# Layer 2 of a fused four-layer graph network: y as two float32r halves, one product of 256 columns per block

## The reference, cut to what matters

```
edge_emb = edge_attr @ We + be
edge_agg = segment_sum(edge_emb, dst, num_segments=num_nodes)
x_comb = concatenate([x, edge_agg], axis=-1)
neigh = segment_sum(x_comb[src], dst, num_segments=num_nodes)
h = x_comb + neigh
return relu(h @ W1 + b1) @ W2 + b2
```

## Time and profile before

| | us |
|---|---|
| median of 3 runs | 6356.68 (6347.64 to 6359.1) |
| the profiled execution | 6362.92 |
| its span, first to last instruction | 6357.5 |
| layer 2, first to last product of L1090 | 3405.5 to 4234.8 |
| first gather of layer 3 | 4248.8 |

### The profile page before, as it was taken

The page is one execution under the profiler, slowest core; times in us unless marked ns, Lnnn a source line. Parts: engine busy times, 40 slices in busy tenths (PEclk is TensorE's granted clock), DMA queues, the critical chain, the costliest instruction groups (busy, mean ns, idle before and its releaser), DMA issues.

```text
span 6357.5 us, 76532 instructions
## 1 busy us (share of the span) xinstructions
PE 5116.0 (80%) x25981; PEld 3920.8 (62%) x25981; DVE 2600.6 (41%) x10082; ACT 1910.0 (30%) x3903; POOL 3110.5 (49%) x3243
## 2 busy tenths in 40 slices
PE   6999999989999999999999999974454444444454
PEld 4777777757777777777776888854444444444344
DVE  7777777623333333333332111113343444434344
ACT  5777777622222222222222111111111111111112
POOL 0000000067777777777770000027777777777775
PEclk8999999999999999999999999987777777777777
DMA  3333322367777666666663555532222222222221
GB/s 135 126 126 126 125 121 122 126 199 210 207 207 209 204 203 204 207 203 203 205 205 116 179 179 177 177 112 54 55 55 54 55 55 54 55 54 55 54 55 44
DMA packets 466448, 844.29 MB, mean 133 GB/s; under 512 B 72324, under 2 KB 300212, under 8 KB 454548
## 3 DMA queue, kind: packets, MB, share of 16 engines
q1 hardware_dynamic: 322996, 509.22, 23.7%
q0 software_dynamic: 128960, 320.44, 18.3%
q10 hardware_dynamic: 14112, 9.74, 0.5%
HBM read 683.93 MB, written 155.18 MB: 132 GB/s over the span
## 4 chain that ended last, share of the span: by engine, by line
PE 65%; POOL 19%; issue 7%; DVE 4%; DMA 2%; ACT 2%; ACTq 0%; SPq 0%; POOLq 0%; DVEq 0%
POOL ring L485 19%; PE bank L970 16%; PE bank L1090 11%; PE bank L957 10%; PE bank L662 10%; PE bank L646 4%; PE bank L531 3%; DMA ring<-htab,src 2%; PE bank L1363 1%; PE bank L1399 1%; PE bank L1392 1%; PE bank L897 1%; PE bank L1370 1%; DVE ring L1294 1%; PE bank L894 1%
## 5 line engine op out<-in xcount | busy, mean ns | idle before, releaser
L485 POOL DMA_INDIRECT ring<-ptab,src x1612 | 1525.0, 946 | 1810.2 <-DMA ptab<-pO 1285.2
L485 POOL DMA_INDIRECT ring<-htab,src x1612 | 1580.9, 981 | 1398.8 <-DMA htab<-hs 907.9
L970 PE MATMUL bank<-ring,oh 128*126 128x384 f32 x3224 | 1218.8, 489 | 0.0
L926 DVE TENSOR_TENSOR ring<-bank,ring 128x512 f32<-128x512 f32 x806 | 553.0, 691 | 1397.1 <-PE bank L957 1150.2
L957 PE MATMUL bank<-w1e,ea 128*128 128x256 f32 x3224 | 833.4, 381 | 16.4 <-DVE ring L926 10.1
L940 ACT ACTIVATE ring<-ring 128x1024 f32<-128x1024 f32 x403 | 425.5, 1056 | 1229.0 <-DVE ring L926 1229.0
L957 PEld LDWEIGHTS bank<-w1e,ea 128*128 128x128 f32 x3224 | 614.4, 191 | 279.1 <-DVE ring L926 19.9
L1355 PE MATMUL bank<-ident,pk 128*72 128x128 f32 x90 | 38.3, 426 | 883.0 <-ACT pk L1317 883.0
L970 PEld LDWEIGHTS bank<-ring,oh 128*126 128x126 f32 x3224 | 590.3, 188 | 218.6 <-issue 0.6
L1399 PE MATMUL bank<-ring,oh 128*126 128x132 f32 x3224 | 576.1, 313 | 174.0 <-DVE ring L1294 171.7
L1399 PEld LDWEIGHTS bank<-ring,oh 128*126 128x126 f32 x3224 | 486.5, 213 | 254.6 <-DVE ring L1294 233.3
(11 more groups left out here) (254 smaller groups left out, 5865.3 us busy)
## 6 DMA issues: line engine op xcount, KB each, us to landing
ring<-ea_r SPq DMA_DIRECT2D x403, 256.0 KB, 4.0
ea<-ea_t SPq DMA_DIRECT2D x403, 256.0 KB, 3.1
atab<-ring SPq DMA_DIRECT2D x45, 1543.5 KB, 5.2
atab<-at SPq DMA_DIRECT2D x45, 1543.5 KB, 5.2
ring<-atab SPq DMA_DIRECT2D x54, 787.5 KB, 4.3
ring<-atab SPq DMA_DIRECT2D x54, 756.0 KB, 4.2
at<-atab SPq DMA_DIRECT2D x36, 787.5 KB, 4.3
at<-atab SPq DMA_DIRECT2D x36, 756.0 KB, 4.1
```

What stands on the lines that cost most here:

```text
L485: return e.indirect_dma_start(o, None, table, bass.IndirectOffsetOnAxis(ap=src[:, t:t + 1], axis=0))
L926: e.tensor_tensor(group1(gi, m % 2), MLP[m % 3][:, :].rearrange("p (g f) -> p g f", g=2), group1(gi, m % 2), ALU.add).then_inc(s_edge, 1)
L970: e.matmul(SUM[s % 2][0:SL, 0:384], slots_of(s, i), rv1[:, t // G % NR1, t % G, :], start=i == 0, stop=t == END[s]).then_inc(s_sum1, 1)
```

## The change

Layer 2 alone is changed.

- y is written as two halves of 12 bits in float32r, `yhl`, 256 columns of a block. `split2` does it on DVE alone, three instructions for each of the nine chunks: u = 4097 y - y, hi = 4097 y - u (rounded), lo = y - hi. Before it was two on DVE and two on ACT.
- Each of the 4410 products has 256 columns for 384, and both its operands are float32r.
- The adjacency is loaded in three parts of 17, 17 and 15 blocks, still bf16, into four buffers `adjb`, and each part is copied to float32r in one of three buffers `adj`: 270 copies. `by_vector` gives the odd ones from the fifth on to DVE (133), the others to ACT (137). A copy stands 11 places ahead of its first product. It waits for its load and for the last product of the part three before it. The load of a part waits for the copy of the part four before it.
- A group is kept with one ACT copy of 128 columns (for 256) and one DVE sum (for two).
- The new buffers lie over `ring`, `oh` and beyond, so that POOL clears `oh` (128 x 4788) behind the last sum of layer 2 (`pool2`), ahead of its gathers for layer 3, and DVE waits for that before layer 3.

```diff
@@ -115,8 +115,10 @@
     CMID = S * NB // 2
     CB = 6
     NCB = -(-NB // CB)
-    HALF = -(-NB // 2)
-    NAT = 5
+    THIRD = -(-NB // 3)
+    PARTS = [min(THIRD, NB - THIRD * k) for k in range(3)]
+    NAT = 4
+    SPLIT = 4097.0
     assert max(LAST[t] - FIRST[t] for t in range(NT)) <= 1 and max(B1[s] - B0[s] for s in range(NS)) <= 1
     assert (NRING * G) % GT == 0
     END = [min(GT * s + GT, NT) - 1 for s in range(NS)]
...
@@ -195,6 +195,10 @@
         flag = sb("flag", [P, 8])
         flagi = sb("flagi", [1, 1], I32)
         gidx = sb("gidx", [P, 2], I32)
+        held = sb("held", [P, ND, 384])
+        gathering = ExitStack()
+        ring = sb("ring", [P, NRING * G * HROW], c=gathering)
+        oh = sb("oh", [P, 2, GT * (SL + S)], c=gathering)
...
@@ -449,6 +454,13 @@
             w3h = sb("w3h", [P, 3, 4], c=l3)
             part = sb("part", [P, 2, P], c=l3)
             l3.close()
+            gathering.close()
+            halves2 = ExitStack()
+            yhl = sb("yhl", [P, NB, 256], FR, c=halves2)
+            adj = sb("adj", [P, 3, THIRD * SL], FR, c=halves2)
+            adjb = sb("adjb", [P, NAT, THIRD * SL], BF, c=halves2)
+            over = sb("over", [P, 2, CB * P], c=halves2)
+            halves2.close()
...
@@ -978,23 +987,58 @@
             N2, _, NODES2, KEEPS2, ADDS2, W2 = places(
                 0, (8, 14, 20, 26, 32, 33, 34, 35, 36, 42, 48, 54, 60, 62), GT, 64)
 
+            def by_vector(u):
+                return u > 3 and u % 2 == 1
+
+            def full2(u):
+
+                v = by_vector(u)
+                return s_full2v if v else s_full2a, sum(by_vector(w) == v for w in range(u + 1))
+
+            FULL2 = {}
+            for u in range(3 * NS):
+                FULL2.setdefault(max(0, GT // 3 * u - 11), []).append(u)
+
+            def pool2(e):
+
+                e.wait_ge(s_sum2, 3 * NS)
+                e.memset(oh[:, :, :], 0.0).then_inc(s_clear2, 1)
+
             def sync2(e):
                 e.wait_ge(s_sum1, NT)
                 e.wait_ge(s_mlp, 2 * NG)
-                for u in range(2 * NS):
+                for u in range(3 * NS):
                     if u >= NAT:
-                        e.wait_ge(d2.sum, u - NAT + 1)
-                    c, n = u % 2 * HALF * SL, (HALF if u % 2 == 0 else NB - HALF) * SL
-                    e.dma_start(PARTS[u % NAT][:, 0:n], atab[u // 2 * P:(u // 2 + 1) * P, c:c + n]).then_inc(
+                        e.wait_ge(*full2(u - NAT))
+                    c, n = u % 3 * THIRD * SL, PARTS[u % 3] * SL
+                    e.dma_start(adjb[:, u % NAT, 0:n], atab[u // 3 * P:(u // 3 + 1) * P, c:c + n]).then_inc(
                         s_part2[u % NAT], 16)
 
-            def y2(b):
-                return hs[:, b, 0:128]
+            def part_ready(e, u):
+                e.wait_ge(s_part2[u % NAT], 16 * (u // NAT + 1))
+                if u >= 3:
+                    e.wait_ge(s_sum2, u - 2)
+                n = PARTS[u % 3] * SL
+                return adj[:, u % 3, 0:n], adjb[:, u % NAT, 0:n]
+
+            def split2(e, c):
+
+                b = slice(CB * c, min(CB * c + CB, NB))
+                y, hi, lo = hs[:, b, 0:128], yhl[:, b, 0:128], yhl[:, b, 128:256]
+                u = over[:, c % 2, 0:(b.stop - b.start) * P].rearrange("p (b f) -> p b f", f=P)
+                e.wait_ge(s_yout1, b.stop)
+                if c >= 2:
+                    e.wait_ge(s_split2, 3 * c - 4)
+                e.scalar_tensor_tensor(out=u, in0=y, scalar=SPLIT, in1=y, op0=ALU.mult, op1=ALU.subtract).then_inc(s_split2, 1)
+                e.wait_ge(s_split2, 3 * c + 1)
+                e.scalar_tensor_tensor(out=hi, in0=y, scalar=SPLIT, in1=u, op0=ALU.mult, op1=ALU.subtract).then_inc(s_split2, 1)
+                e.wait_ge(s_split2, 3 * c + 2)
+                e.tensor_tensor(lo, y, hi.bitcast(F32), ALU.subtract).then_inc(s_split2, 1)
 
             def vector_post2(e, b, k):
                 n, x, o = 5 * b, xs[:, b, :], tail1(b)
                 if k == 0:
-                    e.wait_ge(d2.add, b + 1)
+                    e.wait_ge(s_add2, b + 1)
                     if b:
                         e.wait_ge(s_turn2, b)
                     e.tensor_tensor(mS[:, 0:128], acc1(b, 128), hs[:, b, 0:128], ALU.add).then_inc(s_in2, 1)
...
@@ -1056,22 +1100,33 @@
             def vector2(e):
                 e.wait_ge(s_sum1, NT)
                 for q in range(N2):
-                    dense_split_v(e, d2, q, y2)
+                    if q < NCB:
+                        split2(e, q)
+                    for u in FULL2.get(q, []):
+                        if by_vector(u):
+                            e.tensor_copy(*part_ready(e, u)).then_inc(s_full2v, 1)
                     if q - 1 in KEEPS2:
-                        thirds_added(e, d2, KEEPS2[q - 1])
+                        s = KEEPS2[q - 1]
+                        h = held[0:SL, s % ND, :]
+                        e.wait_ge(s_low2, s + 1)
+                        e.tensor_tensor(h[:, 128:256], SUM[s % 2][0:SL, 0:128], h[:, 0:128], ALU.add).then_inc(s_kept2, 1)
                     if q in NODES2:
-                        node_hots(e, NODES2[q], d2.node, d2.add, ND, B1[max(0, NODES2[q] - ND)] + 1)
+                        node_hots(e, NODES2[q], s_node2, s_add2, ND, B1[max(0, NODES2[q] - ND)] + 1)
                     for b, k in W2.get(q, []):
                         vector_post2(e, b, k)
 
             def scalar2(e):
                 e.wait_ge(s_sum1, NT)
                 for q in range(N2):
-                    if q % 2 == 0 and q // 2 < NCB:
-                        e.wait_ge(s_yout1, min(CB * (q // 2) + CB, NB))
-                    dense_split_a(e, d2, q, y2)
+                    for u in FULL2.get(q, []):
+                        if not by_vector(u):
+                            e.activation(*part_ready(e, u), ACT.Copy).then_inc(s_full2a, 1)
                     if q in KEEPS2:
-                        thirds_kept(e, d2, KEEPS2[q], 384, 2 * KEEPS2[q] + 2)
+                        s = KEEPS2[q]
+                        e.wait_ge(s_sum2, 3 * s + 3)
+                        if s >= ND:
+                            e.wait_ge(s_add2, B1[s - ND] + 1)
+                        e.activation(held[0:SL, s % ND, 0:128], SUM[s % 2][0:SL, 128:256], ACT.Copy).then_inc(s_low2, 1)
                     for b, k in W2.get(q, []):
                         scalar_post2(e, b, k)
 
@@ -1080,19 +1135,19 @@
                 for q in range(N2):
                     g, i = q // GT, q % GT
                     for h in range(NB * i // GT, NB * (i + 1) // GT) if g < NS else ():
-                        u, c = 2 * g + h // HALF, h % HALF
+                        u, c = 3 * g + h // THIRD, h % THIRD
                         if c == 0:
-                            e.wait_ge(s_part2[u % NAT], 16 * (u // NAT + 1))
+                            e.wait_ge(*full2(u))
                         if h == 0 and g >= 2:
-                            e.wait_ge(d2.kept, 2 * (g - 1))
+                            e.wait_ge(s_kept2, g - 1)
                         if g == 0 and h % CB == 0:
-                            e.wait_ge(d2.lo, 2 * (h // CB) + 2)
-                        m = e.matmul(SUM[g % 2][0:SL, 0:384], PARTS[u % NAT][:, c * SL:c * SL + SL], ysp[:, h, 0:384],
+                            e.wait_ge(s_split2, 3 * (h // CB) + 3)
+                        m = e.matmul(SUM[g % 2][0:SL, 0:256], adj[:, u % 3, c * SL:c * SL + SL], yhl[:, h, :],
                                      start=h == 0, stop=h == NB - 1)
-                        if h in (HALF - 1, NB - 1):
-                            m.then_inc(d2.sum, 1)
+                        if c == PARTS[u % 3] - 1:
+                            m.then_inc(s_sum2, 1)
                     for b in LASTS.get(ADDS2.get(q), []):
-                        add_nodes(e, b, 128, 128, d2.node, d2.kept, 2, s_in2, 1, d2.add)
+                        add_nodes(e, b, 128, 128, s_node2, s_kept2, 1, s_in2, 1, s_add2)
                     for b, k in W2.get(q, []):
                         tensor_post2(e, b, k)
 
...
@@ -1283,6 +1338,7 @@
 
             def vector3(e):
                 e.wait_ge(s_hout2, NB)
+                e.wait_ge(s_clear2, 1)
                 for u in range(NS + 8):
...
@@ -1400,7 +1456,7 @@
                                      stop=t == END[g]).then_inc(s_sum3, 1)
 
             with nc.Block() as block:
-                block.gpsimd(lambda e: [f(e) for f in (pool1, pool3)])
```

More of the change, by code:

```diff
@@ L146, in build @@
         atab = nc.dram_tensor("atab", [NS * P, NB * SL], BF)
-        ring = sb("ring", [P, NRING * G * HROW])
         src = sb("src", [P, NT], I32)
@@ L159, in build @@
         npcol = sb("npcol", [P, NB])
-        oh = sb("oh", [P, 2, GT * (SL + S)])
         oh2 = sb("oh2", [P, ND, 256])
@@ L405, in expected @@
             s_eat = [sem(f"s_eat{i}") for i in range(NEA)]
-            d0, d2 = (Dense(*(sem(f"s_{n}{i}") for n in Dense._fields)) for i in (0, 2))
```

(21 more changed lines are left out.)

## The result

| | before | after |
|---|---|---|
| median, us | 6355.3 (4 runs, 6347.64 to 6359.1) | 6166.6 (4 runs, 6165.89 to 6168.08) |
| span of the profiled execution, us | 6357.5 | 6160.6 |
| layer 2, first to last product, us | 829.3 | 635.5 |
| last product to first gather of layer 3, us | 14.0 | 18.15 |

The changed kernel takes 0.9705 of the time before, with a 95% interval of 0.9688 to 0.9722: 189 us less by the medians, 197 by the two profiled spans. The forecast was 6132 us. A second set of four runs on another chip gave 0.9700 (0.9684 to 0.9716).

A forecast was written before the change was run, and what follows sets the result against it. PE alone was taken to bound layer 2: products -237, opening +1, steps and weights +11 make -225 us from the profiled 6362.9, so 6138; the median 6.2 lower, 6132 us. Range 6105 to 6210.

The forecast's parts named there:

- one pass with small stalls: Forecast's main case for layer 2: float32r products in one pass and few waits, 6105 to 6162 us; chance 67%.
- (d): Rival: layer 2's copies and block steps bind, by stalls of 40 us and a slower DVE cast: 6162 to 6192 us; 11%.
- (e): Rival: layer 2's transfers bind, if 210 to 230 GB/s is the most: 6166 to 6225 us; 6%.
- The product: Layer 2's 4410 products: one float32r pass of 110 ns in place of 163.7, saving 237 us.
- (a): Rival: a float32r product in layer 2 costs two passes, 217 ns: +235 us, 6592 us; 7%.
- (b): Rival: weight load isn't hidden and alternates with the product in layer 2, 219 ns: +244 us, 6601 us; 3%.
- (c): Rival: float32r is done as f32 in layer 2, 434 ns a product: +1192 us, 7549 us; 4%.
- The weights: Loads of 4-byte weights in layer 2 run beside a 110 ns product: 0 to +2 ns each, 1 us allowed.
- The opening: Layer 2's start, DVE splitting y: +1 us (0 to +4); the line's waits should show 15 to 20 us.
- Copies and stalls: Layer 2's copies: 1.98 us on ACT, 1.27 on DVE; block steps behind them cost PE about 10 us (0 to 40).
- The transfers: Layer 2's adjacency loads at 245 GB/s, a DMA share of 0.74: hidden, +0.
- The end: Last product to layer 3's first gather, 14.0 us: POOL's 4.9 us clearing hidden; without cover 5 us.

The follow-up runs named there:

- e4_bf256: The kernel before with bf16 products of 256 columns for 384 in layer 2: 109.3 ns a product, layer 592.6 us, kernel 6120.5 us.
- e3_w64: The changed kernel with 64 columns of weights for 126 in layer 2's products: 118 ns to the next piece, layer 628.5 us for 635.5.
- e2_192: The changed kernel with layer 2's float32r products at 192 columns for 256: 110 ns between neighbours, layer 599.8 us.
- e11_192w64: The changed kernel with 192 columns for 256 and 64 columns of weights for 126 in layer 2's products: 89 ns, layer 525.5 us.
- e5_pitch: The changed kernel with each block's 126 weight columns on a pitch of 128 in the buffers: 117.5 ns for 118.2, layer 642.1 us.
- e1_384: The changed kernel with layer 2's float32r products at 384 columns for 256: 175 ns between neighbours, layer 884.4 us, kernel 6413.5 us.
- e6_nocopy: The changed kernel with only the first three parts of the adjacency loaded and copied, then used again: layer 634.6 us for 635.5.

## Why the prediction was right, and where it was off

- **The range.** It holds the result in part by luck. The forecast's own case, one pass with small stalls, was given 6105 to 6162, and 6166.6 lies outside that. The range went on to 6210 only for rivals (d) and (e), and neither came about. What filled it was a product 8 ns too long, which no case had, less some terms that were put too high.
- **What bounds.** Right. PE was the whole of layer 2, and 194 of the 197 us came from there.
- **The product.** One pass by its rate, and rivals (a), (b) and (c) fall: no 217, 219 or 434 ns. The reason that was given for one pass, that both operands come already cut to 12 bits, no run tests. And the term was mis-sized. 110 ns is what bf16 takes (e4_bf256); float32r takes 118.4. 4410 x 0.0084 = 37 us, which is more than the whole error of 35. The step that failed is "160 ns for 384 columns and 3.7 ns over, so 256 columns would be 106.7 + 3.7 = 110 ns": it carried bf16's rate over to a form that has its own, and the bounds around it came from pass counts, with nothing between 108 and 217.
- **The weights.** Right to within what matters: load and product run side by side, 1 us was allowed and e3_w64 shows 1.6 ns a product at most, 7 us, for half the load. The load alone needs 110 ns (e2_192 against e11_192w64). The rule of the Trainium skill that rival (b) names stands in "TensorE: Matmul & The Clock Gate" under "The mechanism", just ahead of the section given; 118.4 ns for product and load on the same rows speak against it as the earlier trace rows do.
- **The opening.** +1 us forecast, +0.4 measured. The 19.2 us read from the earlier trace rows as the wait for the split were 9.5 of PE and 9.7 of the loads; the sum didn't use them, but the sign "15 to 20 us" did, and PE's wait is 11.8. Each wait of an instruction on the one before it cost 0.04 us (0.3 us in eight).
- **Copies and stalls.** The durations were right to 1%. The 10 us for steps that wait behind copies were too much: PE shows no wait for them in any of the 49 blocks. Rival (d) falls for this kernel, but what it describes is real: with a cast of 2.4 us PE waits 5.9 us (e5_pitch), and with products of 89 ns it is idle for 9.4 us in 480, half of it for such a step (e11_192w64).
- **The transfers.** Hidden, as forecast: share 0.75 for 0.74. e11_192w64 moves 285 GB/s at a share of 0.88 over 200 us, so the 210 to 230 of rival (e) are no limit.
- **The end.** Forecast hidden, "without that cover it would be 5 us". It cost 4.2. The clearing was priced nearly right (4.9 us forecast, 4.09 measured) and its cover was judged by the engine alone: POOL was free, but its clearing held up DVE, on the path.

Sum: against the profiled executions the gain was 197 us, and 225 were forecast, 28 too many. 37 of the difference are the product, 4 the end, 3 the products of group 0, which wait for the split whatever they take (49 x 0.0537 = 2.6 us that were counted as saved), and 3 PE's other work (1.10 us a group for 1.06). The other way go 11 for stalls and weights that didn't come, 1 for the opening and 7 in the layers that didn't change. The last 7 of the 35 us lie outside the sum: the median was put 6.2 us below the profiled execution, and stood 0.7 above it (6166.6 and 6165.89).

Open is why a column of float32r takes 5% longer than one of bf16 (0.445 against 0.425 ns) and each product some 4 ns more, at a granted clock of 1.00 in every window of layer 2. It isn't the load (e1_384, e3_w64), the address but for 0.7 ns (e5_pitch), nor traffic beside it (e6_nocopy). The f32 records, with operands as wide, don't show it (217 ns for two passes of 256 columns), so that the width alone isn't it either.

## What to carry to other kernels

When a number format is new to a trace, time one product of it, or let the range hold a rate a few per cent off the format next to it: 8 ns of a product that is done 4410 times were the larger part of the error here. A large sum with whole-number weights may be worth writing in two 12-bit halves for float32r rather than three of 8 bits for bf16, as long as its product stays longer than the load of its weights. A long instruction on an idle POOL is not free: look at which DVE instruction stands beside it.

## What the runs showed of the hardware

- float32r products follow each other in 118.4, 175 and 232.3 ns for 256, 384 and 512 columns: one pass, 0.445 ns a column and 4.5 ns. bf16's take 109.3 and 163.7 for 256 and 384. With 192 columns float32r's stay at 110 ns, which is the load of 126 columns of weights; with 64 columns of weights they come to 89.
- A DVE cast from bf16 to float32r of 2142 elements takes 1273 ns in one run of elements, and 2381 ns when it writes 17 runs of 126 on a pitch of 128; ACT's takes 1996 and 1998.
- A DVE cast of 768 elements from f32 to float32r takes 553 ns, against 951 and 958 for the two instructions with 4097 in whose place it was put. That it rounds to 12 bits as they do is not shown.
- A clearing of 4788 elements takes 4.09 us on POOL and 4.05 on DVE. On POOL it stretched a 128x128 DVE instruction from 0.34 to 3.49 us.
